# Sixteen-head stablemax attention on one core: one clip in five on VectorE, one plan step later copies, first keys on two queues, clearing after a norm

## The reference

```python
s = where(x >= 0, x + 1.0, 1.0 / (1.0 - x))            # stablemax, s / sum(s)
q, k, v = query @ Wq.T + bq, key_value @ Wk.T + bk, key_value @ Wv.T + bv   # 154 keys, 16 heads of 16
scores = einsum('bhqd,bhkd->bhqk', q, k) / sqrt(HD)
x = x + tanh(g_xattn[0]) * (stablemax(scores) @ v) @ Wo.T + bo      # layernorm(x) is the query
x = x + tanh(g_ffn[0]) * moe(layernorm(x))             # 64 experts, top 8, capacity 128, and a shared one
x = x + tanh(g_xattn[1]) * softmax_attention(layernorm(x), ctx)
x = x + tanh(g_ffn[1]) * butterfly_mlp(layernorm(x))
```

## Time and profile before

| what | us |
|---|---|
| median of 3 runs (range) | 1233.26 (1229.75 to 1236.8) |
| the profiled execution | 1231.84 |
| its span | 1229.6 |
| PE busy | 1034.0 |
| DVE busy | 817.2 |
| ACT busy | 702.2 |

### The profile page before, as it was taken

The page is one execution under the profiler, slowest core; times in us unless marked ns, Lnnn a source line. Parts: engine busy times, 40 slices in busy tenths (PEclk is TensorE's granted clock), DMA queues, the critical chain, the costliest instruction groups (busy, mean ns, idle before and its releaser), DMA issues.

```text
span 1229.6 us, 17473 instructions
## 1 busy us (share of the span) xinstructions
PE 1034.0 (84%) x5635; PEld 751.7 (61%) x5635; DVE 817.2 (66%) x2051; ACT 702.2 (57%) x1351; POOL 360.6 (29%) x313
## 2 busy tenths in 40 slices
PE   4688888888876688998899976888898989899888
PEld 2354544544444577887687755657676767767567
DVE  4468778777778766755667658687567577664543
ACT  1899878988975433565554421364455455544542
POOL 2000000000000003778777631124334251423223
PEclk9779988988887888999999996899999999999998
DMA  6564435434121323788988644331312133120000
GB/s 145 122 153 137 129 95 167 120 82 129 52 73 69 128 61 104 184 203 199 245 198 184 146 119 92 88 109 26 106 46 80 37 104 82 50 56 1 20 18 18
DMA packets 97401, 128.41 MB, mean 104 GB/s; under 512 B 26976, under 2 KB 69344, under 8 KB 97056
## 3 DMA queue, kind: packets, MB, share of 16 engines
q1 hardware_dynamic: 82448, 105.73, 30.0%
q0 software_dynamic: 12288, 18.88, 8.5%
q10 hardware_dynamic: 2576, 2.69, 1.0%
HBM read 66.15 MB, written 30.70 MB: 79 GB/s over the span
## 4 chain that ended last, share of the span: by engine, by line
PE 51%; DVE 26%; ACT 9%; issue 6%; POOL 3%; DMA 2%; SPq 2%; ACTq 2%; DVEq 0%; POOLq 0%
PE psum L912 6%; PE psum L1098 6%; PE psum L1083 5%; PE psum L1001 4%; PE psum L928 4%; PE psum L819 3%; DVE stats L1363 3%; PE psum L795 3%; PE psum L865 3%; PE psum L1030 2%; DVE weights L1484 2%; DVE peaks L1764 2%; PE psum L960 2%; PE psum L741 2%; DVE normed L1404 2%
## 5 line engine op out<-in xcount | busy, mean ns | idle before, releaser
L1863 POOL TENSOR_SCALAR vareps<-moments 128x4 f32<-128x4 f32 x32 | 10.4, 326 | 529.2 <-DVE moments L1366 529.2
L795 PE MATMUL psum<-q_stack,k_stack 96*128 96x512 f32 (+1 forms) x256 | 123.2, 511 | 39.2 <-DVE weights L1484 24.8
L1297 ACT ACTIVATE weights<-psum 128x512 f32<-128x512 f32 x160 | 94.1, 597 | 71.7 <-PE psum L795 60.7
L1484 DVE SCALAR_TENSOR_TENSOR weights<-psum,weights 128x512 f32<-128x512 f32 x160 | 102.5, 681 | 43.2 <-ACT weights L1162 43.0
L1883 POOL DMA_INDIRECT expert_sums<-made,sum_rows x64 | 105.4, 1647 | 59.3 <-DVE made L1734 38.6
L1910 POOL TENSOR_TENSOR hidden<-hidden_whole,hidden 128x512 fp32r<-128x512 f32 x64 | 82.3, 1287 | 114.2 <-DVE hidden L1812 114.2
L1030 PE MATMUL psum<-k_stack,q_stack 96*128 96x256 f32 x256 | 88.2, 395 | 31.9 <-DVE peaks L1764 20.0
L1764 DVE TENSOR_REDUCE peaks<-psum 128x2 f32<-128x308 f32 x256 | 107.0, 469 | 12.1 <-PE psum L1032 11.6
L912 PE MATMUL psum<-feat_parts,w_shared_up 128*128 128x512 f32 x384 | 100.5, 412 | 10.7 <-DVE shared_silu L1608 6.3
L1098 PE MATMUL psum<-w_con_high,hidden 128*128 128x256 f32 x512 | 102.2, 298 | 0.1
L1812 DVE CAST hidden<-hidden_whole 128x512 fp32r<-128x512 f32 x64 | 52.7, 823 | 71.6 <-ACT hidden_whole L1326 70.3
(11 more groups left out here) (211 smaller groups left out, 2390.9 us busy)
## 6 DMA issues: line engine op xcount, KB each, us to landing
expert_w<-in_expert_w SPq DMA_DIRECT2D x64, 384.0 KB
q_stack<-q_stage SPq DMA_DIRECT2D x96, 128.0 KB, 3.0
q_stack<-q_stage SPq DMA_DIRECT2D x174, 64.0 KB, 2.0
expert_sums<-zeros SPq DMA_DIRECT2D x6, 1408.0 KB, 8.2
fetched<-expert_sums SPq DMA_DIRECT2D x16, 512.0 KB, 4.8
rows_scratch<-rows SPq DMA_DIRECT2D x8, 640.0 KB, 3.4
k_raw<-in_k SPq DMA_DIRECT2D x16, 300.0 KB
x<-in_x SPq DMA_DIRECT2D x8, 512.0 KB, 4.8
```

Of the source, the lines that this page charges most:

```text
L795: T.matmul(to, k[0:row, head_at(head), :], q[0:row, head // 2, :], start=True, stop=True).then_inc(scored, 1)
L1297: A.activation(weights1[n % 6][:, :], score_bank[n % 2], ACT.Exp).then_inc(exped, 1)
L1484: V.scalar_tensor_tensor(weights[n % 9][:, :], score_bank[n % 5], 1.0, weights[n % 9][:, :], ALU.add, ALU.max).then_inc(weighted, 1)
```

## The change

- `clip_last`: the fifth chunk's clip is a DVE `tensor_scalar` (times -1, maximum with 0) in place of ACT's Relu. It stands in the list one iteration ahead, behind the `weight`s of the iteration before it. It has a semaphore of its own.
- `after_steps` gets an empty entry between `turn_att` and `att_feats`; all later entries come one place later.
- The first keys: ACT sends places 0 and 1; SP sends the queries of places 0 and 1, and then queries and keys of place 2, and of place 3.
- GpSimd's clearing of buffers at the start waits until the first norm has been written.
- Two semaphores of loads are joined into one (`gating_in`).

```diff
 def after_steps(h):
-    return [turn[0:2], divide[0:2] + turn[2:4], divide[2:4], [("turn_att", h)], [("att_feats", h)],
+    return [turn[0:2], divide[0:2] + turn[2:4], divide[2:4], [("turn_att", h)], [], [("att_feats", h)],
...
         if 0 <= i - 1 < len(sets):
             plan += [("weight", n) for n in sets[i - 1]]
+        if i + 1 < len(sets) and len(sets[i + 1]) == 1:
+            plan.append(("clip_last", sets[i + 1][0]))
...
-        plan += [("clip", n) for n in now]
+        if len(now) > 1:
+            plan += [("clip", n) for n in now]
         step()
...
-                    to_key_stack(A, 0)
+                    to_key_stack(A, 0, (0, 1))
...
             def log(n):
-                A.wait_ge(clipped, n + 1)
+                if n % 5 == 4:
+                    A.wait_ge(clipped_last, n // 5 + 1)
+                else:
+                    A.wait_ge(clipped, n // 5 * 4 + n % 5 + 1)
...
+            def clip_last(n):
+                if n >= 9:
+                    V.wait_ge(weighed, weighed_by(n - 9))
+                V.wait_ge(scored, n + 1)
+                V.tensor_scalar(weights[n % 9][:, :], score_bank[n % 5], -1.0, 0.0, ALU.mult,
+                                ALU.max).then_inc(clipped_last, 1)
...
             def clear_rest():
+                G.wait_ge(ln_normed, HT)
...
             def send_q(h):
-                send(S, q_stage, q_stack[h % 2][:, :, :], q_in[h % 2])
+                together = (0, 1) if h == 0 else range(4)
+                send(S, q_stage, q_stack[h % 2][:, :, :], q_in[h % 2], places=together)
+                if h == 0:
+                    S.wait_ge(keys_split, 1)
+                    for r in (2, 3):
+                        send(S, q_stage, q_stack[0][:, :, :], q_in[0], places=(r,))
+                        to_key_stack(S, 0, (r,))
```

More of the change, by code:

```diff
@@ L662, in build @@
         x_in, ident_in, gates_in, wq_in, bk_in = sems("x_in", HALVES), sem("ident_in"), sem("gates_in"), sem("wq_in"), sem("bk_in")
-        wv_in, bo_in, wo_in, gate_w_in, upper_in = (sem(f"{n}_in") for n in ("wv", "bo", "wo", "gate_w", "upper"))
+        wv_in, bo_in, wo_in, gating_in = (sem(f"{n}_in") for n in ("wv", "bo", "wo", "gating"))
         ctx_in, wk_in, wk_laid, k_in, q_in = sem("ctx_in"), sem("wk_in"), sem("wk_laid"), *(
@@ L678, in build @@
             sem(n) for n in ("dve_own", "ln_bn", "ln_stats", "ln_normed", "bias_set"))
+        clipped_last = sem("clipped_last")
         keys_split, queries_split, weighted, masked, rows_set, summed = (
@@ L703, in weighed_by, with send @@
             return 2 * (n // 5) + 1 + (n % 5 == 4)
-        def send(engine, stage, stack, landed, parts=((0, 0), (0, 32), (1, 64))):
+        def send(engine, stage, stack, landed, parts=((0, 0), (0, 32), (1, 64)), places=range(4)):
             hi, st = stage[:, :, :, :].bitcast(F32), stack.bitcast(F32)
-            for r in range(4):
+            for r in places:
                 for part, row in parts:
@@ L726, in wait_all, with to_key_stack @@
                 engine.wait_ge(landed[r], 48 * times)
-        def to_key_stack(engine, b):
+        def to_key_stack(engine, b, places=range(4)):
             send(engine, k_stage, k_stack[b % 2][:, :, :].rearrange("p (n a) k -> p n (a k)", a=3), k_in[b % 2],
-                 ((0, 0), (1, 32), (0, 64)))
+                 ((0, 0), (1, 32), (0, 64)), places)
         def tensor_program(T):
@@ L874, in gate @@
                 if h == 0:
-                    T.wait_ge(gate_w_in, 16)
+                    T.wait_ge(gating_in, 32)
                 T.wait_ge(*misc.freed(("turn_rows", h), CD - 1))
@@ L886, in count @@
                 if h == 0:
-                    T.wait_ge(upper_in, 16)
+                    T.wait_ge(gating_in, 32)
                     T.wait_ge(pool_set, POOL_FIRST)
@@ L1828, in vector_program @@
             units = {"stats": stats_, "norm": norm, "key_mask": key_mask, "bias_parts": set_bias_parts, "key_rest": key_rest,
-                     "set_values": set_values, "q_parts": q_parts, "weight": weight,
+                     "set_values": set_values, "q_parts": q_parts, "clip_last": clip_last, "weight": weight,
                      "divide": divide, "x_add": x_add, "shift": shift, "top": top_, "pick": pick,
@@ L1960, in load_rest @@
                 S.dma_start(wo[:, :, :], D["wo"]).then_inc(wo_in, 16)
-                S.dma_start(gate_w[:, :, :], D["gate_w"]).then_inc(gate_w_in, 16)
-                S.dma_start(upper[:, :], D["upper"]).then_inc(upper_in, 16)
+                S.dma_start(gate_w[:, :, :], D["gate_w"]).then_inc(gating_in, 16)
+                S.dma_start(upper[:, :], D["upper"]).then_inc(gating_in, 16)
             def send_keys(b):
```

## The result

| | before | after |
|---|---|---|
| median of 4 runs each (range), us | 1233.36 (1229.75 to 1236.8) | 1254.32 (1251.81 to 1256.84) |
| ratio, 95% interval | | 1.0178 (1.0146 to 1.021) |
| profiled execution, its span, us | 1231.84, 1229.6 | 1251.81, 1250.2 |
| granted clock | 0.927 | 0.914 |

The changed kernel is slower by 21 us. The forecast said slower, 1242, with a range that ends at 1253: the direction held, the size did not.

What follows compares the result with a forecast made beforehand. The prediction took ACT and DVE as full, with each half's loop closed through DVE and PE. -6.5 - 2.4 + 3 x 4.7 + 2 x 3.4 - 0.3 - 2.0 + 0.3 = +10.0 on 1231.84; forecast 1242, range 1224 to 1253.

Steps and rivals of the forecast that it cites:

- The start: Kernel start: ACT's first clip 5.9 us earlier, first norm 1.1 us quicker, SP's later sends +0.5; -6.5 us with the norm.
- What closes a half: Each half: its loop closes through DVE and PE, with ACT's full queue beside it and 3.4 us to spare.
- the view that ACT alone is the bound: Rival reading, whole kernel: the clips leaving ACT save 20.8 us and the start 6.5, giving 1204; faster in all, chance 0.25.
- The clip's price: Fifth chunk's clip on DVE: 0.60 us each, three a half ahead of the three weights, 1.8 us.
- The five halves with queries: Middle halves: the empty place and clips add 4.7 us in three, 3.4 in the two that also project keys.
- "-0.3" for the half after the last queries: Half without `turn_q`: four clips save 2.6 us, waits of `keep` and `row_feats` cost 0.7 and about 1.6.
- "-2.0" for the end: At the end: the last `keep`'s weigh now stands ahead of `count`; about -2.0 us for clip, order and waits together.
- the gate's bank: Halves with queries: the gate, now behind `turn_q`, waits for `q_feats` to read a bank until 20.8 us; DVE idles 2.9.
- the floor: Half with queries, every wait gone: DVE would reach the three weights at 33.8 us, 0.8 later than before.
- First stretch: Up to the first `att_feats`: five clips save 3.2 us on ACT, `turn_att`'s arrival takes back about 0.8; -2.4.
- Tail: Tail of the list: one place more, +0.3 us.
- the ceiling: Halves with queries: PE's clock falls in the waits, one 0.9 us weigh slowdown three times a half adds 2.5 us.

Runs made afterwards that it cites:

- start_only: Changed kernel without the empty place and with every clip on ACT, so only the sends and the clearing are changed: 1225.83 us, ratio 0.9942.
- clip_and_start: Changed kernel without the empty place, its clips on DVE and its start kept: 1233.77 us, ratio 1.0013.
- place_only: Kernel before with only the empty place between `turn_att` and `att_feats` added: 1251.27 us, ratio 1.0143.
- place_behind_gate_exp: Kernel before with one empty place between `gate_exp` and `top`, so only `top` and later entries move: 1242.3 us, ratio 1.0082.
- place_late_first: Kernel before with the empty place ahead of `att_feats` and the three streams taken in the order late, keyed, early: 1251.71 us, ratio 1.0168.
- start_clips_q_parts: Changed kernel without the place; DVE clips in the first four groups only; from the second half's queries, their first splitting operation on ACT: 1221.22 us, ratio 0.9907.

## Why the prediction was right in direction and wrong in size

**Right.** *The start.* Told -6.5, measured -7.0 at the first clip (28.28 for 35.30), the norm 1.38 us as told, start_only -6.8 by the medians. The last keys were issued by 32.47 + 1.88 = 34.4 us, where they were told to land near 39, since SP needed only 0.63 us for each once it sent alone. *What closes a half.* DVE and PE, not ACT: ACT's work fell by 13.2 us and nothing came of it, and the view that ACT alone is the bound (1204) was wrong by 50 us. *The clip's price.* Told 0.60 us each; DVE's work grew by 15.6 for 28, 0.56 each. *The waits by name*, in the third half: gate behind `q_feats` 2.09 us, `shift` 4.01 (told 2.9), `row_feats` 1.88 (told 2.0; 1.9 to 3.0 in the first five). The gate, told to start at 20.8 us, started at 20.97, 22.16 and 21.79 in halves 1, 3 and 5. In the halves with keys `shift` waited 0.4 us only. *The five halves with queries.* Told 3 x 4.7 + 2 x 3.4 = 20.9, measured 4.2 + 2.8 + 6.1 + 5.1 + 5.0 = 23.1.

**The step that failed: "-0.3" for the half after the last queries and "-2.0" for the end.** They came as +4.6 and +3.9, 10.8 us off, as much as the whole miss (told +10, measured +20.7 between the spans). That the two agree so well is luck in part: the other terms are off by -0.5, +1.4, +2.2 and -3.2, and cancel. I let four clips save 2.6 us there because they leave ACT. In the same text I had written that a half is closed through DVE; with no `turn_q` to wait for I dropped that and counted ACT. DVE's side of the walk needs no `turn_q`: `project_o` behind two scores and a weigh, the second `x_add` at 7.4 us instead of 5.96, the clips at 0.6 each. I had worked that out for the halves with queries and left it out here. DVE's second `x_add` and the norm of the routed rows in half 6, before (`att_feats` at 302.17) and after (317.20), at a granted clock of 1.00 in both:

```profile
308.12 0.75 DVE L1505 SCALAR_TENSOR_TENSOR x<-psum,tanh_gates,x 128x512 f32<-128x512 f32 x1 [1.18 <-PE psum L865]
...
312.23 1.38 DVE L1404 TENSOR_SCALAR rows<-x,moments,rstd 128x256 f32<-128x256 f32 x4 [0.47 <-POOL rstd L1868]
```

```profile
325.50 0.75 DVE L1519 SCALAR_TENSOR_TENSOR x<-psum,tanh_gates,x 128x512 f32<-128x512 f32 x1 [1.60 <-PE psum L869]
...
331.27 1.38 DVE L1411 TENSOR_SCALAR rows<-x,moments,rstd 128x256 f32<-128x256 f32 x4 [0.46 <-POOL rstd L1882]
```

The second `x_add` comes at 8.30 us instead of 5.95, the norm at 14.07 instead of 10.06, and `pick` at 26.15 instead of 22.21: 3.9 of the half's 4.6 us. In half 7 `pick` comes at 25.94 instead of 22.19, 3.8 of its 3.9. By the parts, clip_and_start has +0.8 and +2.2 in these two halves, place_only +1.6 and +1.6, place_behind_gate_exp +2.4 and +0.7. ACT in half 6 of the changed kernel shows what became of the saving, waits of 1.3, 0.7, 1.8 and 2.2 us:

```profile
326.82 0.60 ACT L1176 ACTIVATE turned<-psum 128x512 f32<-128x512 f32 x1 [1.28 <-PE psum L818]
...
328.08 0.63 ACT L1165 ACTIVATE weights<-weights 128x512 f32<-128x512 f32 x1 [0.66 <-DVE weights L1493]
...
334.19 0.60 ACT L1127 ACTIVATE row_feats<-psum 128x512 f32<-128x512 f32 x1 [1.78 <-PE psum L745]
...
357.20 0.60 ACT L1176 ACTIVATE turned<-psum 128x512 f32<-128x512 f32 x1 [2.19 <-PE psum L818]
```

At the end the last `keep`, told to come 2 us sooner, comes 382.95 - 357.70 = 25.25 us after `att_feats` instead of 364.47 - 338.08 = 26.39, 1.1 sooner. But `att_feats` follows it 14.8 us later and not 9.7. An earlier `keep` is of no use there: DVE works from `top` to `position` without a gap until 388.7 and comes only then to `divide` and the token lists' first tile, for which ACT waits 7.05 us, where it waited 3.43 (before, `position` ended at 365.3, under 1 us after `keep` had begun). Before, then after:

```profile
368.49 0.72 ACT L1254 ACTIVATE numbered<-hot_a,token_numbers 128x512 f16<-128x512 bf16 x1 [3.43 <-DVE hot_a L1690]
```

```profile
390.59 0.72 ACT L1261 ACTIVATE numbered<-hot_a,token_numbers 128x512 f16<-128x512 bf16 x1 [7.05 <-DVE hot_a L1704]
```

**Right in part by luck.** I charged the halves with queries to the gate's bank. The wait exists, but without it (place_late_first) place and order together still cost 16.5 us, and a place that leaves the gate alone costs 10.6. What the runs show is the amount of time in which DVE has nothing to do, 83.5 to 85.7 us in each of the four kernels whose `gate` and later entries come a place later on the code of before, whatever name the wait has. The price of the place in halves with queries was therefore near the mark by a walk that ended in one wait, and it is not shown that this wait is its cause.

**Smaller terms.** From the second `x_add` to the three weights I had read 24.57 us of work out of DVE's named waits; the window has 23.97, since the timeline names no cause for its smallest gaps. That number entered the floor alone. First stretch told -2.4, measured 50.23 - 51.24 = -1.0 between first clip and first `att_feats`. Tail told +0.3, measured -2.9. Both lie within what executions of the same code differ by (51.88 and 55.32, 854.5 and 862.0). The clock was told as the ceiling, not in the sum; it did fall, 0.90 to 0.83 in the seven halves, and PE took 12.2 us more for the same matmuls. How much of the 31.6 us that is isn't shown: it is the whole +2.2 in half 7 of clip_and_start, and nothing of the 4.0 us by which the norm is late in half 6 here.

**Open.** The place costs 10.6 us behind `gate_exp` and 18.7 behind `turn_att` by the medians. That the other 8 come in at the gate and at `x_add` is suggested by the row between them (15.1 by the medians, 1.0106), but the intervals overlap. Nor was PE's clock held apart from the waits: place_behind_gate_exp has 0.88 and 8.1 us in the halves, the four kernels with the place further ahead 0.83 to 0.84 and 17.1 to 19.8. Why the halves with keys lose nothing to a late `top` (-1.0 and -0.1) was not tested.

## What to carry to other kernels

Find the engine through which the loop closes and write the loop's length as its work plus its idle time, over the whole loop, from one row of busy times. That sum sizes the cost of an edit even when the waits change their names, though it does not say what caused the idle time. A walk along that engine must be made for every part of the loop, also where the wait that was looked at is missing. Work moved from an engine that looks full to the one that closes the loop costs its own duration, less what falls into gaps (here 15 us of clips cost 8, part of it through PE's clock, and 7 us moved the other way gave 4). In a list that all engines walk in order, making a chain later is not free because each piece still fits: work that filled a gap early comes back late, in front of what closes the loop.

## What the runs showed of the hardware

- A `tensor_scalar` between SBUF tiles beside GpSimd's memsets took 2.19 and 2.44 us for four, without them 1.38. The Trainium skill ("SBUF — State Buffer", section on who interferes with whom) says that VectorE and GpSimd share a pair of ports, and that while one holds it (VectorE in its two-port modes, which a `tensor_scalar` between SBUF tiles can enter) the other waits for the whole instruction. These numbers agree with such a wait, but which mode the norm ran in is not shown. At the first clip the difference was 0.7 us.
- Issue of a transfer took 0.92 us on SP and 1.03 on ACT with both sending twelve (10.98 and 12.37 us), 0.87 and 1.01 with nine and six (7.85, 6.05), and 0.63 once SP sends alone (1.89 for three).
- The clip on DVE, a `tensor_scalar` from PSUM with two constants, took 685 ns for 512 columns, for the 744 of the earlier trace rows: nothing near the 0.40 us that the prediction held possible. Told was 0.60 by the pace of the weights, and DVE's work did grow by 0.56 each, less than a row's duration, since neighbours overlap.

```profile
L1493 DVE TENSOR_SCALAR weights<-psum 128x512 f32<-128x512 f32 x32 | 21.9, 685 | 2.4 <-PE psum L802 2.4
```

- PE's gate, 16 matmuls of 128x65, took 1.90 us at a granted clock of 1.00 (2.4 GHz) and 3.51 at 0.50 (1.2 GHz).
- ACT's Identity with a bias, from PSUM, took 687 ns where DVE took 744 for the same operation (start_clips_q_parts, ACT's group).

```profile
L1160 ACT ACTIVATE q_stage<-psum,bq 128x512 fp32r<-128x512 f32 x14 | 9.6, 687 | 2.8 <-PE psum L788 2.7
```
